# Token stage of a fused vision and text layer: filter taps stacked on the contraction rows, and four pairs of images as one run of 28 tiles

## The chip, the cores and the metric

The kernel runs on one core of a Trainium2 chip, as one program. The metric is the device time of one execution in microseconds. The profile is of one execution of the same program and lists the instructions of each engine: PE is TensorE's matmul (PEld its weight load), DVE is VectorE, ACT is ScalarE, POOL is GpSimd, and SP is SyncE, which here issues DMAs.

## The reference

Eight images of 64 channels and 56x56 pixels are turned into tokens. A patch of 3x3 taps is gathered round each pixel, gated by a small network of its own, and projected. 128 text tokens are put behind the 3136 image tokens, and one layer of causal attention (8 heads of 8, 4 key/value heads, rotary positions) and of a feed-forward block that half the tokens go through follows.

```python
t = unfold3x3(x)                                  # [8, 3136, 64*9]
h1 = relu(t @ W1 + b1)                            # 576 -> 64
s = sigmoid(h1 @ W2 + b2)                         # 64 -> 576
h = concat([(t * s) @ W3 + b3, txt], axis=1)      # 576 -> 64; [8, 3264, 64]
h = h + attention(layernorm(h), Wq, Wk, Wv, Wo)
h = h + feed_forward(layernorm(h), ...)
```

## The kernel before, in words

The program is a row of stages with a barrier between them: `tokens`, `attention`, `inverse_sums`, `second_norm`, `select` and `feed_forward`. Only `tokens` and the arrays that it reads are touched. It makes `h`, its layer norm, and queries, keys and values for attention.

**Data.** Two images form a pair: the 64 channels of each lie on 128 partitions. A loop (`Fori`) runs the pairs, four in all, and inside a pair the code runs seven tiles of 8 image rows, which are 448 tokens. Each convolution tap is a matmul of 128 contraction rows by 128 output rows by 448 columns in f32, with a block-diagonal weight: image one in one quarter, image two in the opposite one, and zeros in the other two. The trace shows an f32 matmul as two MATMUL instructions.

**One tile on PE.** Nine hidden products (`w1_sb`, L419) add up in `hidden_ps`; ACT makes `h1` of it (Relu, L469). Nine gate products (`w2_sb`, L433) go one after the other into the two slots of `gate_ps`; ACT turns each into a tanh (L475), DVE multiplies it with the shifted image (L507, `gated`), and a token product (`w3_sb`, L446) adds it into `token_ps`. Gate products are issued three ahead of the token products. When all nine are in, PE waits for its own last product and tells DVE, which takes the tile into `h0` (L492).

**What follows a tile** is called a post: `product_stage`, `activation_stage`, `vector_stage` and `sum_and_rest`. PE centres the tile (L271), ACT squares it (L303), PE averages (L275), ACT takes the root (L308), DVE the reciprocal (L324) and the normalised tile (L326). PE makes queries and keys, each once straight and once turned (L284), DVE multiplies them with cosine and sine (L338, `rot`). POOL adds the two (L371, `full`), ACT casts the sum to bf16 (L317), POOL takes the rest (L378), ACT casts that too, and POOL takes the last rest (L382): three bf16 parts, which SP stores with twelve DMAs (`store_parts`, L260). Values are made of 128 tokens at a time (L293) and copied by DVE (L355). The post of a tile is done within the tile that comes after it, at places written out by hand in `POST_AT`: centring and average between the nine hidden products, queries and keys between the gate products. The root needs another function table on ACT than tanh, so the tables are changed twice a tile (ACT_TABLE_LOAD at L308 and L475).

**Round a pair.** The text tokens are turned first (L410), and their post is put between the stages of the first tile. At the end of a pair DVE copies the next pair's images, loaded in the meantime, into the padded `x_pad` (L525); all engines meet at a barrier, SP clears the semaphores, and they meet again. The last post of a pair is done in the first tile of the next; the last of all stands behind the loop.

## Time and profile before

| | us |
|---|---|
| median of 3 runs (lowest, highest) | 5276.06 (5275.87, 5278.95) |
| the profiled execution, its own time | 5275.56 |
| its span, first to last instruction | 5274.0 |
| PE busy | 4587.6 (87%) |
| DVE busy | 4049.6 (77%) |
| ACT busy | 3538.7 (67%) |
| POOL busy | 629.6 (12%) |
| `tokens`, until the first instruction of `attention` | 928.2 |

PE is called busy from a matmul's start to its modelled end, and matmuls overlap, so sums of their durations say more than there is; the distance from one start to the next is what a matmul costs. The page gives TensorE's granted clock, of which there are two levels, 2.4 GHz (1.00) and 1.2 GHz (0.50). A timeline row merges instructions of one kind that follow each other; its second number is the time from the first's start to the last's end.

### The profile page before, as it was taken

What the parts mean: (1) busy time and instruction counts of PE and PEld (TensorE: products, weight loads), DVE (VectorE), ACT (ScalarE), POOL (GpSimd) and SP (SyncE); (2) the same over time, 40 slices, a digit from 0 to 9 for tenths busy, and PEclk for the clock granted to TensorE, in tenths of its full rate; (3) what the DMA queues carried; (4) which work ended last, traced back from release to release, by engine and by line L of the source; (5) the groups of instructions that cost most, each with busy time, mean ns of one, the idle gap of its engine ahead of it and who ended that gap; (6) DMA issues with size and microseconds to landing.
All of it is one profiled execution on the core that took longest, in us unless ns stands there. A gap on an engine that the chain in (4) does not pass through costs nothing. (4 is left out here: it accounts for less than half of the span.)

```text
span 5274.0 us, 109173 instructions
## 1 busy us (share of the span) xinstructions
PE 4587.6 (87%) x42956; PEld 1660.9 (31%) x42956; DVE 4049.6 (77%) x4595; ACT 3538.7 (67%) x7169; POOL 629.6 (12%) x1092
## 2 busy tenths in 40 slices
PE   8898987499999989999998999999899999965466
PEld 3444433133333333333333333333233333321222
DVE  5555555689989979998997999899799989965511
ACT  3343433088888878888886888888788888842133
POOL 2222222010010001001001000100100010012100
PEclk9999999599999989999998999999899999977688
DMA  3222122200010010001001000100100010024233
GB/s 109 68 68 70 56 64 61 77 15 8 8 36 8 8 31 14 8 6 37 10 6 33 12 8 6 36 10 6 35 10 8 6 38 8 6 69 140 67 105 102
DMA packets 168631, 194.27 MB, mean 37 GB/s; under 512 B 53644, under 2 KB 128572, under 8 KB 167228
## 3 DMA queue, kind: packets, MB, share of 16 engines
q1 hardware_dynamic: 168132, 187.49, 12.6%
q8 instruction: 329, 5.39, 0.4%
q14 instruction: 170, 1.39, 0.1%
HBM read 105.18 MB, written 81.36 MB: 35 GB/s over the span
## 5 line engine op out<-in xcount | busy, mean ns | idle before, releaser
L792 DVE TENSOR_REDUCE part_max<-max_scores 128x2 f32<-128x1024 f32 (+3 forms) x3096 | 3228.9, 1101 | 369.5 <-PE max_scores L750 267.0
L920 ACT ACTIVATE probs<-scores 128x512 f32<-128x512 f32 (+4 forms) x6272 | 2996.3, 538 | 547.7 <-PE scores L950 442.0
L974 PE MATMUL out_acc<-probs,v_keys 128*32 128x256 f32 (+2 forms) x23424 | 1789.8, 378 | 0.0
L750 PE MATMUL max_scores<-k_rows,q_rows 48*128 48x512 bf16 (+5 forms) x6416 | 1147.6, 370 | 184.2 <-DVE part_max L792 114.5
L950 PE MATMUL scores<-q_rows,k_rows 50*128 50x512 bf16 (+4 forms) x6272 | 1218.3, 354 | 90.3 <-ACT probs L920 45.4
L900 POOL TENSOR_SCALAR_AFFINE_SELECT probs<-probs 128x256 f32<-128x256 f32 (+1 forms) x832 | 336.1, 404 | 3418.4 <-ACT probs L920 3415.9
L750 PEld LDWEIGHTS max_scores<-k_rows,q_rows 48*128 48x128 bf16 (+1 forms) x6416 | 302.9, 94 | 1296.8 <-DVE part_max L792 757.6
L974 PEld LDWEIGHTS out_acc<-probs,v_keys 128*32 128x32 f32 x23424 | 463.0, 108 | 737.2 <-issue 624.0
L950 PEld LDWEIGHTS scores<-q_rows,k_rows 50*128 50x128 bf16 x6272 | 469.8, 94 | 434.3 <-ACT probs L920 227.5
L507 DVE SCALAR_TENSOR_TENSOR gated<-gate,x_pad 128x448 f32<-128x448 f32 x252 | 260.8, 1073 | 68.9 <-ACT gate L475 56.0
L446 PE MATMUL token_ps<-gated,w_sb 128*128 128x448 f32 x504 | 234.7, 556 | 32.9 <-DVE gated L507 32.9
L433 PE MATMUL gate_ps<-h,w_sb 128*128 128x448 f32 x504 | 231.7, 560 | 18.0 <-ACT h L469 14.5
L475 ACT ACTIVATE gate<-gate_ps,b_sb 128x448 f32<-128x448 f32 x252 | 154.9, 631 | 110.7 <-PE gate_ps L433 106.2
L324 DVE RECIPROCAL rstd<-std 128x448 f32<-128x448 f32 (+1 forms) x33 | 89.5, 2711 | 178.9 <-ACT std L308 178.9
L757 PE MATMUL max_scores<-masks_sb 64*128 64x128 bf16 (+2 forms) x3424 | 220.1, 207 | 0.0
L419 PE MATMUL hidden_ps<-x_pad,w_sb 128*128 128x448 f32 x504 | 212.9, 559 | 3.6
L1555 DVE SCALAR_TENSOR_TENSOR scaled<-y_ps,ff_b_sb,chosen 128x512 f32<-128x512 f32 (+1 forms) x28 | 19.7, 702 | 217.6 <-PE y_ps L1502 217.6
L1513 PE MATMUL hidden_ps<-normed,ff_w_sb 128*128 128x512 f32 (+1 forms) x224 | 113.9, 659 | 81.3 <-DMA chosen<-chosen_dram 81.3
L757 PEld LDWEIGHTS max_scores<-masks_sb 64*128 64x128 bf16 (+1 forms) x3424 | 163.2, 98 | 43.8 <-issue 5.1
L1542 ACT ACTIVATE hidden<-hidden_ps,ff_b_sb 128x512 f32<-128x512 f32 (+1 forms) x112 | 71.5, 649 | 150.5 <-PE hidden_ps L1513 150.5
L371 POOL TENSOR_TENSOR full<-rot 128x448 f32<-128x448 f32 (+1 forms) x66 | 69.0, 1046 | 669.2 <-DVEq L342 669.2
L446 PEld LDWEIGHTS token_ps<-gated,w_sb 128*128 128x128 f32 x504 | 88.8, 189 | 153.8 <-DVE gated L507 95.1
(122 smaller groups left out, 1980.0 us busy)
## 6 DMA issues: line engine op xcount, KB each, us to landing
q_terms_dram<-q_st SPq DMA_DIRECT2D x174, 112.0 KB
q_rows<-q_terms_dram SPq DMA_DIRECT2D x180, 96.0 KB, 2.2
v_keys<-v_blocks_dram SPq DMA_DIRECT2D x18, 832.0 KB, 9.4
v_blocks_dram<-v_st SPq DMA_DIRECT2D x26, 512.0 KB, 3.4
k_rows<-k_terms_dram SPq DMA_DIRECT2D x36, 306.0 KB, 6.7
k_terms_dram<-k_st SPq DMA_DIRECT2D x174, 56.0 KB
x_in<-in_x SPq DMA_DIRECT2D x5, 1568.0 KB, 6.1
h_dram<-h SPq DMA_DIRECT2D x28, 224.0 KB, 2.0
```

The costliest lines, as they stand in the source:

```text
L419: last = nc.tensor.matmul(hidden_ps[:, 0, 0:CT], w1_sb[:, s], x_pad[:, r0 + i:r0 + i + IMG_ROWS, j:j + W], start=(s == 0), stop=(s == SHIF ...
L433: nc.tensor.matmul(gate_ps[:, g % 2, 0:CT], w2_sb[:, s], h1[:], start=True, stop=True).then_inc(gate_ready, 1)
L446: last = nc.tensor.matmul(token_ps[:, 0, 0:CT], w3_sb[:, s], gated[:, g % GATE_RING], start=(s == 0), stop=(s == SHIFTS - 1))
L475: nc.scalar.activation(gate[:, g % GATE_RING], gate_ps[:, g % 2, 0:CT], ACT.Tanh, bias=b2_sb[:, s:s + 1], scale=0.5).then_inc(tanh_ready, 1)
L507: nc.vector.scalar_tensor_tensor(out=gated[:, g % GATE_RING].rearrange("p (h w) -> p h w", h=IMG_ROWS), in0=gate[:, g % GATE_RING].rearran ...
L750: last = nc.tensor.matmul(max_scores[to:to + m, n % M_RING, v, 0:keys], q_rows[rows, g, p, q0:q0 + m], k_rows[rows, (u // BU) % STEP_B, g, ...
L757: last = nc.tensor.matmul(max_scores[to:to + m, n % M_RING, v, keys - m + HALF * half:keys], masks_sb[rows, 1 + 2 * half, 0:m], masks_sb[r ...
L792: nc.vector.tensor_reduce(part_max[0:m, u % 2, i, :, p, c], max_scores[0:m, n % M_RING, :, 0:keys], AX_X, ALU.max).then_inc(max_used, 1)
L900: nc.gpsimd.affine_select(block_probs, block_probs, [[0, GKV], [1, keys]], ALU.is_ge, 0.0, base=0, channel_multiplier=-1).then_inc(p_maske ...
L920: nc.scalar.activation(probs[0:keys, k % P_RING, s, o:width[t]], scores[0:keys, (GH * k + s) % S_RING, o:width[t]], ACT.Exp, scale=float(H ...
L950: nc.tensor.matmul(scores[0:keys, n % S_RING, o:width[t]], k_rows[rows, u // BU, g, j * P:j * P + keys], q_rows[rows, g, p, begin[t] + o:b ...
L974: last = nc.tensor.matmul(out_acc[VW * s:VW * s + VW, lo:hi], v_keys[0:keys, u // BU, g, j, v * VW:(v + 1) * VW], probs[0:keys, k % P_RING ...
```

## The change

Everything after `tokens` is left as it is. In `tokens`:

- **Taps on the contraction rows.** Of the three taps of a filter row, the first two are stacked: `x_taps` holds, for each image, 64 channels on the lower partitions and the same channels one pixel further on the upper ones. A hidden or token product of these two taps is one matmul per image with 128 contraction rows and 64 output rows, the two images in the two halves of the output; a gate product is one per image with 64 contraction rows and 128 output rows. The third tap of each filter row stays as it was, block-diagonal for both images (`x_both`). A tile has six units: units 0 to 2 are such a couple of matmuls, units 3 to 5 one whole matmul each. The number of matmuls, tanh or sigmoid activations and gate multiplications is 9 of each as before.
- **Order.** The loop over pairs, the barriers, the clearing of semaphores and the copy into the padded image are gone; 28 tiles are written out. In a tile, unit by unit, PE issues the gates of the unit, hidden products of the next tile, token products of the unit before, and a stage of a post. A post is spread over the two tiles behind its own: `posts(n, u)` and `norms(n, u)` say what of it stands where. The text is turned in the fourth tile of a pair; its post stands there and in the fifth.
- **Gate.** The sigmoid is taken as such (L570) and not as a tanh, and DVE multiplies it with the image in a TENSOR_TENSOR (L624).
- **Loads.** The padded image comes from the host's array. SP loads it in pieces of 8 rows, five DMAs a piece, each as soon as the tile that used the old rows is done; the weights are loaded by 19 DMAs from ACT's queue.

```diff
+UNITS_T = 2 * KS
+TEXT_AT = 3
...
+        x_both = sbuf("x_both", [P, PH, PW])
+        x_taps = sbuf("x_taps", [P, 2, PH, PW])
...
+        h1 = sbuf("h1", [P, 2, CT])
...
+        def late(n):
+
+            return 1 if n % CTILES == TEXT_AT + 1 else 0
+
+        def posts(n, u):
+
+            at = []
+            if n >= 2 and u == 0:
+                at.append((POST_OF[n - 2], 3))
+            if n >= 1 and u in (1 + late(n), 2 + late(n), 5):
+                at.append((POST_OF[n - 1], {1: 0, 2: 1}.get(u - late(n), 2)))
+            if n % CTILES == TEXT_AT and u == 5:
+                at.append((text_post(n), 0))
+            if late(n) and u < 3:
+                at.append((text_post(n), u + 1))
+            return at
+
+        def norms(n, u):
+
+            if n >= 1 and u == 3 + late(n):
+                return [POST_OF[n - 1]]
+            return [text_post(n)] if late(n) and u == 0 else []
...
+        def gate_ops(u):
+            return [2 * u, 2 * u + 1] if u < KS else [KS + u]
+
+        def load_rows(eng, p, n):
+
+            r0, r1 = n * IMG_ROWS, (n + 1) * IMG_ROWS if n < CTILES - 1 else PH
+            a, b = r0 * PW, r1 * PW
+            eng.dma_start(x_both[:].rearrange("p h w -> p (h w)")[:, a:b], x[p][:, a:b]).then_inc(piece_loaded[n], 16)
+            for e in range(2):
+                flat = x_taps[:, e].rearrange("p h w -> p (h w)")
+                for half in range(2):
+                    eng.dma_start(flat[C * half:C * (half + 1), a:b],
+                                  x[p][C * e:C * (e + 1), a + half:b + half]).then_inc(piece_loaded[n], 16)
...
-        with nc.Fori(0, PAIRS) as p:
...
-                        for s in range(SHIFTS):
-                            i, j = divmod(s, KS)
-                            last = nc.tensor.matmul(hidden_ps[:, 0, 0:CT], w1_sb[:, s],
-                                                    x_pad[:, r0 + i:r0 + i + IMG_ROWS, j:j + W],
-                                                    start=(s == 0), stop=(s == SHIFTS - 1))
-                            if s in POST_AT["hidden"]:
-                                product_stage(pe, due(n), POST_AT["hidden"].index(s))
...
-            nc.all_engine_barrier(sem_only=True)
-            for s in step_sems:
-                nc.sync.sem_clear(s)
...
+                for n in range(1, NT + 1):
+                    pair, i = (n - 1) // CTILES, (n - 1) % CTILES
+                    store_h0(sp, taken_before(n - 1), pair, i * CT, CT)
+                    if pair + 1 < PAIRS:
+
+                        sp.wait_ge(hidden_ready, n)
+                        sp.wait_ge(gated_ready, SHIFTS * n)
+                        load_rows(sp, pair + 1, i)
...
+                    if u < KS:
+                        for e in range(2):
+                            last = nc.tensor.matmul(hidden_ps[C * e:C * (e + 1), 0:CT], w1p_sb[:, u],
+                                                    x_taps[:, e, r0 + u:r0 + u + IMG_ROWS, 0:W],
+                                                    start=(u == 0), stop=False, skip_group_check=True)
+                    else:
+                        row = r0 + u - KS
+                        last = nc.tensor.matmul(hidden_ps[:, 0:CT], w1b_sb[:, u - KS],
+                                                x_both[:, row:row + IMG_ROWS, 2:2 + W],
+                                                start=False, stop=(u == UNITS_T - 1), skip_group_check=True)
...
+                    for s in gate_ops(u):
+                        g = n * SHIFTS + s
+                        if g >= 2:
+                            pe.wait_ge(sigmoid_ready, g - 1)
+                        if u < KS:
+                            e = s % 2
+                            nc.tensor.matmul(gate_ps[:, g % 2, 0:CT], w2p_sb[C * e:C * (e + 1), u],
+                                             h1[C * e:C * (e + 1), n % 2], start=True, stop=True).then_inc(gate_ready, 1)
+                        else:
+                            nc.tensor.matmul(gate_ps[:, g % 2, 0:CT], w2b_sb[:, u - KS], h1[:, n % 2],
+                                             start=True, stop=True).then_inc(gate_ready, 1)
...
+                    for s in gate_ops(u):
+                        g = n * SHIFTS + s
+                        pe.wait_ge(gated_ready, g + 1)
+                        if u < KS:
+                            e = s % 2
+                            last = nc.tensor.matmul(token_ps[C * e:C * (e + 1), 0:CT], w3p_sb[:, u],
+                                                    gated[:, g % GATE_RING], start=(u == 0), stop=False,
+                                                    skip_group_check=True)
+                        else:
+                            last = nc.tensor.matmul(token_ps[:, 0:CT], w3b_sb[:, u - KS], gated[:, g % GATE_RING],
+                                                    start=False, stop=(u == UNITS_T - 1), skip_group_check=True)
+                        last.then_inc(gated_used, 1)
+                    if u == UNITS_T - 1:
+                        pe.wait_ge(gated_used, (n + 1) * SHIFTS)
+                        nc.tensor.sem_inc(token_ready, 1)
...
+                for n in range(NT):
+                    for u in range(UNITS_T):
+                        gates(n, u)
+                        if n + 1 < NT:
+                            for h in ((0, 1), (2,), (3,), (4,), (5,), ())[u]:
+                                hidden(n + 1, h)
+                        if u >= 1:
+                            if u == 1 and n % CTILES == TEXT_AT:
+                                turn_text(n)
+                            out_tokens(n, u - 1)
+                        elif n >= 1:
+                            out_tokens(n - 1, UNITS_T - 1)
+                        if u == 0:
+                            value_products(pe, n)
+                        for m, stage in posts(n, u):
+                            product_stage(pe, m, stage)
...
+                def relu(n):
+                    act.wait_ge(hidden_ready, n + 1)
+                    if n >= 2:
+                        act.wait_ge(gate_ready, (n - 1) * SHIFTS)
+                    nc.scalar.activation(h1[:, n % 2], hidden_ps[:, 0:CT], ACT.Relu, bias=b1_sb[:]).then_inc(h1_ready, 1)
...
+                for n in range(NT):
+                    for u in range(UNITS_T):
+                        if u == UNITS_T - 1 and n + 1 < NT:
+                            relu(n + 1)
+                        for s in gate_ops(u):
+                            sigmoid(n, s)
+                        for m, stage in posts(n, u):
+                            if stage <= 1:
+                                activation_stage(act, m, stage)
+                        if n >= 2 and u in (2, 4 - late(n)):
+                            activation_stage(act, POST_OF[n - 2], 2 if u == 2 else 3)
+                        if late(n) and u == 5:
+                            activation_stage(act, text_post(n), 2)
+                        if n >= 1 and late(n - 1) and u == 0:
+                            activation_stage(act, text_post(n - 1), 3)
...
+                    nc.vector.tensor_tensor(gated[:, g % GATE_RING].rearrange("p (h w) -> p h w", h=IMG_ROWS),
+                                            gate[:, g % GATE_RING].rearrange("p (h w) -> p h w", h=IMG_ROWS),
+                                            taps, ALU.mult).then_inc(gated_ready, 1)
...
+                for n in range(NT):
+                    for u in range(UNITS_T):
+                        if u == 0 and n >= 1:
+                            take_up_tile(n - 1)
+                        if u == 0:
+                            value_copies(dve, n)
+                        if u == 1 and n % CTILES == TEXT_AT:
+                            pair, t0, w, idx = POST[text_post(n)]
+                            take_up(idx, t0, w, pair)
+                        for s in gate_ops(u):
+                            gating(n, s)
+                        for m, stage in posts(n, u):
+                            if stage >= 2:
+                                vector_stage(dve, m, stage)
+                        for m in norms(n, u):
+                            vector_stage(dve, m, 1)```

How PE's order moves, first as it was: PE in one tile of the loop, from the first hidden product on (`w1_sb`, `w2_sb`, `w3_sb` are hidden, gate and token weights).

```order
L419 MATMUL hidden_ps<-x_pad,w1_sb 128x448 x2
L271 MATMUL norm_ps<-h0,centre_sb 128x448
L419 MATMUL hidden_ps<-x_pad,w1_sb 128x448 x3
L275 MATMUL norm_ps<-square,mean_sb 128x448
L419 MATMUL hidden_ps<-x_pad,w1_sb 128x448 x4
L433 MATMUL gate_ps<-h1,w2_sb 128x448 x4
L446 MATMUL token_ps<-gated,w3_sb 128x448
L284 MATMUL proj_ps<-normed,wq_sb 128x448 x2
L433 MATMUL gate_ps<-h1,w2_sb 128x448
L446 MATMUL token_ps<-gated,w3_sb 128x448
L433 MATMUL gate_ps<-h1,w2_sb 128x448
L446 MATMUL token_ps<-gated,w3_sb 128x448
```

And PE in units 0 to 2 of a tile now (`p` marks weights of stacked taps, `b` those of the third tap).

```order
L483 MATMUL gate_ps<-h1,w2p_sb 128x448 x2
L461 MATMUL hidden_ps<-x_taps,w1p_sb 64x448 x4
L511 MATMUL token_ps<-gated,w3b_sb 128x448
L307 MATMUL proj_ps<-normed,wk_sb 64x448 x2
L483 MATMUL gate_ps<-h1,w2p_sb 128x448 x2
L461 MATMUL hidden_ps<-x_taps,w1p_sb 64x448 x2
L507 MATMUL token_ps<-gated,w3p_sb 64x448 x2
L290 MATMUL norm_ps<-h0,centre_sb 128x448
L483 MATMUL gate_ps<-h1,w2p_sb 128x448 x2
L466 MATMUL hidden_ps<-x_both,w1b_sb 128x448
L507 MATMUL token_ps<-gated,w3p_sb 64x448 x2
L296 MATMUL norm_ps<-square,mean_sb 128x448
```

The nine hidden products no longer stand in a row ahead of the gates; they are those of the next tile and lie between the gates of this one, as does the last token product of the tile before.

ACT in a tile of the loop before, from the square on:

```order
L303 ACTIVATE square<-norm_ps 128x448
L308 ACT_TABLE_LOAD
L308 ACTIVATE std<-norm_ps,eps_sb 128x448
L469 ACTIVATE h1<-hidden_ps,b1_sb 128x448
L475 ACT_TABLE_LOAD
L475 ACTIVATE gate<-gate_ps,b2_sb 128x448 x6
L317 CAST q_st<-full 128x448
L317 CAST k_st<-full 64x448
L475 ACTIVATE gate<-gate_ps,b2_sb 128x448 x2
L317 CAST q_st<-rest 128x448
L317 CAST k_st<-rest 64x448
L475 ACTIVATE gate<-gate_ps,b2_sb 128x448
```

ACT now, from the Relu of the next tile (in unit 5) through units 0 to 4 of that tile:

```order
L562 ACTIVATE h1<-hidden_ps,b1_sb 128x448
L570 ACTIVATE gate<-gate_ps,b2_sb 128x448 x5
L326 ACTIVATE square<-norm_ps 128x448
L570 ACTIVATE gate<-gate_ps,b2_sb 128x448 x2
L333 ACT_TABLE_LOAD
L333 ACTIVATE std<-norm_ps,eps_sb 128x448
L341 CAST q_st<-full 128x448
L341 CAST k_st<-full 64x448
L570 ACT_TABLE_LOAD
L570 ACTIVATE gate<-gate_ps,b2_sb 128x448 x2
L341 CAST q_st<-rest 128x448
L341 CAST k_st<-rest 64x448
```

Both table loads, the root and two casts stood ahead of the first gate or between gates; now they stand in one row between the sixth gate and the seventh.

DVE now, from the taking up of a tile on; before, the reciprocal and the normalised tile stood between the taking up and the first gate multiplication:

```order
L606 TENSOR_SCALAR h0<-token_ps,b3_sb 128x448
L624 TENSOR_TENSOR gated<-gate,x_taps 128x448 x2
L360 TENSOR_TENSOR rot<-proj_ps,cos_sb 64x448
L360 TENSOR_TENSOR rot<-proj_ps,sin_sb 64x448
L624 TENSOR_TENSOR gated<-gate,x_taps 128x448 x4
L624 TENSOR_TENSOR gated<-gate,x_both 128x448
L347 RECIPROCAL rstd<-std 128x448
L349 TENSOR_TENSOR normed<-norm_ps,rstd 128x448
L624 TENSOR_TENSOR gated<-gate,x_both 128x448 x2
L360 TENSOR_TENSOR rot<-proj_ps,cos_sb 128x448
L360 TENSOR_TENSOR rot<-proj_ps,sin_sb 128x448
```

The reciprocal now stands between the seventh gate multiplication and the eighth.

## Rows read from the trace of the kernel before

**Rows 1.** Windows: stretch, us; busy us (instructions) of each engine; clock; DMA share; GB/s.
```profile
0.00:18.30 18.30, 0.45 (x1) 0.19 (x2) 8.71 (x8) 0.68 (x1) 6.31 (x6) 1.00 0.92 343
...
238.50:458.70 220.20, 197.69 (x529) 89.62 (x529) 120.28 (x141) 88.37 (x136) 54.12 (x48) 0.97 0.21 65
...
889.40:928.20 38.80, 11.99 (x32) 5.15 (x32) 10.06 (x20) 4.72 (x7) 6.21 (x6) 0.61 0.26 79
928.20:5274.00 4345.80, 3784.72 (x40816) 1297.69 (x40816) 3553.61 (x4010) 3183.22 (x6622) 400.65 (x888) 0.94 0.11 29
```

**Rows 2.** The same view for one tile of the third pair.
```profile
561.60:590.70 29.10, 27.60 (x75) 12.62 (x75) 16.52 (x17) 11.74 (x19) 7.37 (x6) 1.00 0.16 43
```

**Rows 3.** Timeline of PE there: start, duration of the merged row, idle before it.
```profile
571.02 1.72 PE L284 MATMUL proj_ps<-normed,wk_sb 128*64 128x448 f32 x4
572.67 1.02 PE L433 MATMUL gate_ps<-h,w_sb 128*128 128x448 f32 x2
...
580.31 1.02 PE L446 MATMUL token_ps<-gated,w_sb 128*128 128x448 f32 x2 [0.35 <-DVE gated L507]
581.48 1.74 PE L419 MATMUL hidden_ps<-x_pad,w_sb 128*128 128x448 f32 x4
...
586.82 3.17 PE L419 MATMUL hidden_ps<-x_pad,w_sb 128*128 128x448 f32 x8
589.83 1.89 PE L293 MATMUL proj_ps<-wv_sb,normed 128*128 128x64 f32 x16
```

**Rows 4.** Timeline of PE in attention: output rows of 32, contraction rows of 48 and 50.
```profile
2003.11 0.39 PE L750 MATMUL max_scores<-k_rows,q_rows 48*128 48x512 bf16 x2
2003.34 0.40 PE L950 MATMUL scores<-q_rows,k_rows 50*128 50x512 bf16 x2
2003.67 0.64 PE L974 MATMUL out_acc<-probs,v_keys 128*32 128x256 f32 x8
2004.24 0.39 PE L750 MATMUL max_scores<-k_rows,q_rows 48*128 48x512 bf16 x2
```

**Rows 5.** Timeline of ACT and DVE in the tile of rows 2.
```profile
560.95 0.63 ACT L469 ACTIVATE h<-hidden_ps,b_sb 128x448 f32<-128x448 f32 x1 [2.37 <-PE hidden_ps L419]
561.60 1.28 ACT L475 ACT_TABLE_LOAD   x1
562.90 1.18 ACT L475 ACTIVATE gate<-gate_ps,b_sb 128x448 f32<-128x448 f32 x2
563.56 1.18 DVE L507 SCALAR_TENSOR_TENSOR gated<-gate,x_pad 128x448 f32<-128x448 f32 x2 [1.34 <-ACT gate L475]
...
574.69 0.57 ACT L317 CAST k_st<-full 64x448 bf16<-64x448 f32 x1 [3.70 <-POOL full L371]
575.16 1.15 ACT L475 ACTIVATE gate<-gate_ps,b_sb 128x448 f32<-128x448 f32 x2
575.82 4.44 DVE L507 SCALAR_TENSOR_TENSOR gated<-gate,x_pad 128x448 f32<-128x448 f32 x3 [0.68 <-ACT gate L475]
...
587.69 2.95 DVE L324 RECIPROCAL rstd<-std 128x448 f32<-128x448 f32 x1 [5.54 <-ACT std L308]
```

**Rows 6.** Timeline of POOL and SP beside it.
```profile
576.00 1.41 POOL L378 TENSOR_TENSOR rest<-full,k_st 64x448 f32<-64x448 f32 x1
577.69 2.29 SPq L260 DMA_DIRECT2D k_terms_dram<-k_st  x3
```

**Rows 7.** Timeline of PE behind the last pair, and in `second_norm`.
```profile
897.84 1.85 PE L271 MATMUL norm_ps<-h,centre_sb 128*128 128x448 f32 x2 [8.53 <-PEq L536]
...
4725.01 2.05 PE L1244 MATMUL centred_ps<-h,centre_sb 128*128 128x512 f32 x2 [2.82 <-DVE normed L1226]
...
4765.52 2.08 PE L1236 MATMUL proj_ps<-attn,wo_sb 128*128 128x512 f32 x2 [2.96 <-POOL attn L1179]
```

**Rows 8.** Timeline of the start: SP's first issue, PE's first products.
```profile
0.82 0.40 SPq L141 DMA_DIRECT2D x_in<-in_x  x1
...
18.32 3.32 PE L419 MATMUL hidden_ps<-x_pad,w_sb 128*128 128x448 f32 x4
```

481 lines of the change are left out of this document (239 added, 242 removed).

## The prediction

> **What bounds the kernel now.** I read the windows by stage first [rows 1]. Token stage: 928.2 us, of which 18.3 are a start, 220.2 each of three pairs, 38.8 a tail with the last post, and the rest, 210.5, the last pair. The 4345.8 us behind it are untouched, so the change can only move the 928.2. Inside a pair the window over one tile [rows 2] shows PE busy 27.60 of 29.10 us at clock 1.00, DVE 16.52, ACT 11.74, POOL 7.37: PE bounds the tile.
>
> The timeline gives PE's prices [rows 3]. Eight hidden instructions take 3.17 us with 0.54 for the last one's end, so starts lie 0.376 apart and one f32 product, two instructions, costs a slot of 0.75 us. A tile has 27 + 6 = 33 products: 24.8 us; values and stalls at dependences make up the 29.1. So what is worth most is to have fewer slots.
>
> **Do two half-size products run side by side?** No f32 half product of this size is in the trace, but near ones are [rows 4]. Attention's `out_acc` is f32 with 32 output rows: four products, eight instructions of 256 columns, and the next start is 0.57 us after the first. At 0.376 per 448 columns eight in a row would be 1.72, and two 0.43. So all four lie side by side and 0.14 is lost at the change of shape. For split contraction rows there is only bf16: two `max_scores` of 512 columns, 48 rows each, and the next start is 0.23 later; 512 columns at that pace are 0.21. I take one slot for a couple, both for split outputs (near the `out_acc` row, f32) and split contractions; bounds are one and two slots. Changing shape: four key products with 64 output rows take 1.65 to the next start, against 1.50 for four instructions at that pace [rows 3]: 0.14 for a change in and one out. I take 0.1 a change, bounds 0 and 0.14.
>
> **PE's work now.** Nine couples and nine whole products plus six of the post are 24 slots, 18.0 us. The order changes shape 13 times: 1.3 us. PE's wait for its own last token product stays: 1.17 us from its start to the next [rows 3] in place of 0.75. That is 19.8 us; if PE alone set the pace, a tile would fall by 9 us. It doesn't.
>
> **The path through a tile.** ACT now has two table loads of 1.28, the root and two casts in one row between its sixth and seventh gate, and DVE a reciprocal of 2.95 between its seventh and eighth. I walk a plain tile from its first gate (0), with ACT 0.63 an activation at a pitch of 0.55, casts at a pitch of 0.47, DVE 0.63 at a pitch of 0.55 [rows 5], 0.04 to hand over, and 0.1 more where PE starts out of a wait:
> - PE: gate couple, two hidden couples, last token product with its wait, keys (two), gate couple, hidden couple, token couple, centring: ten slots, 0.42 for the wait, six changes of shape. The third gate couple starts at 8.5.
> - Its first half ends 0.92 after its start; ACT's sixth gate ends at 10.7, table load to 12.0 (PE's average, at 11.1, ends then too), root and two casts to 13.6, table load to 14.9, seventh gate to 15.6.
> - DVE: seventh multiplication to 16.2, reciprocal and normalised tile to 19.8, eighth multiplication to 20.3.
> - PE has run dry meanwhile, 0.5 us ahead of the fourth token unit and 2.6 ahead of the fifth. That starts at 20.45; with the queries (two slots) and a change of shape the next tile starts at 22.8.
>
> So 22.8 us a plain tile, 6.3 less than 29.1. Everything else has room: the casts, Relu and ninth gate end by 18.6; SP issues 12 stores at 0.76 [rows 6] and 5 loads and one more at about 0.4 [rows 8], 11.5 us in all; the loads of the next pair are due six tiles later. Gate multiplications lose their second operation and stay two SBUF inputs; I price the new form like the old.
>
> **Tiles that differ.** Eight blocks of values are 1.8 us of PE (16 instructions, [rows 3]), and keys behind them now wait for DVE's copies of the same slot: +2.2 in two tiles, +3.0 in the tile with the last blocks. Text: +1.2 in the tile that turns it (PE waits for the taking up), +2.7 in the next (another pair of table loads and a reciprocal, partly beside the values), +0.5 behind. A pair is 7 x 22.8 + 7.4 + 4.4 = 171.4 us against 220.2, and has no barrier. The first two tiles have less post: the first pair 157.
>
> **Ends.** Start: ten loads of rows and three of weights instead of everything; I take 10 us, six slots partly at half clock (1.5 us a slot, [rows 8]) and the Relu: 19 until the first gate, bounds 15 and 25. Tail: before, 30.4 us from the last centring at 897.84 [rows 7]. Now ACT casts the post before it, twice, ahead of the last square, which thus stands 8.0 behind the last token product instead of 1.9 behind the centring: 36.5.
>
> **The clock.** Within a tile before, PE was without a running matmul for 1.50 us in all, and the clock stayed at 1.00 [rows 2]. In `second_norm` it idled 2.82 and 2.96 us, and behind each gap it ran at half: matmuls of 512 columns took 2.05 and 2.08 us for two, against 1.00 at full pace, 0.43 and an end of 0.57 [rows 3, 7]. The new gap of 2.6 is nearly as long. All that PE does behind it lies on the path. Stretches at half there held some 3 to 6 us, which cost half their length. I take 1.8 us in every second tile, 25 in all; bounds 0 and 75.
>
> **Sum.** 19 + 157 + 3 x 171.4 + 36.5 + 25 = 751.7 against 928.2: 176.5 less. The profiled execution's own time is 5275.56, so 5099; the median of the runs shown is 0.5 above it. I say **5100 us**.
>
> **The rivals.**
> - *The lock between DVE and POOL.* Three multiplications beside POOL took 4.44 us instead of 1.73 [rows 5], and POOL's 1.0 became 1.41 [rows 6]. In my walk POOL is idle when the seventh and eighth run, by 0.3 us for the seventh. If both meet it, +1.8 a tile: 5150. Chance 0.10.
> - *Gate couples don't overlap.* Each half has its own wait for ACT, and f32 on split contraction rows isn't in the trace. Three slots on the path, 2.25 a tile: 5163. Against it: the bf16 `scores` have such waits too, and two of them take one's time. Chance 0.06.
> - *No couple overlaps: the change doesn't do what it says.* 33 slots again; eight couples lie ahead of the root, 5.9 a tile, and PE has no gap to lose its clock in: 5240. Against it: `out_acc`. Chance 0.04.
> - *A dearer table switch.* In the rows a switch costs the load's 1.28 and the next activation starts at once (561.60 to 562.90, [rows 5]); that is in the sum. The Trainium skill, ScalarE: Activation LUTs, in What ACT_TABLE_LOAD costs, adds a drain of about 1.38 us to each load, which no row here shows. As a mechanism: were there 1.4 us of dead time behind each load only now, when the load follows a busy ACT, two of them a tile on the path are 78 us: 5178. Chance 0.02, since the load at 561.60 follows a Relu directly too.
> - *Slower: PE stays at half clock.* If the clock falls in every gap and doesn't come back within a tile, 24 slots at 1.5 plus the rest are 38 us a tile, and with text and values the stage is near 1175: 5520. It decides from a mean tile of 30 us. Against it: at half clock PE has no gaps left in a tile, and behind each gap of `second_norm` full speed came back. Chance 0.03.
>
> **How the numbers follow.** My forecast, with the clock falling in none to all tiles and changes of shape at 0 to 0.14, is 5060 to 5130 and has 0.73; the rest, 0.02, is that some wait that I don't see eats all of it. The range goes on to take in the lock and the gate couples, and a little below for a walk that is too dear: 5050 to 5165. What a measurement here can tell from no change is 0.2%, 10.6 us. All cases but the last two are faster by more; as the walk has many steps, I leave 0.94 faster, 0.02 same, 0.04 slower.
>
> **What would show it.** Right: two halves of a couple start within some 10 ns of each other in PE's timeline, a slot of 0.75 to the next; from Relu to Relu 22 to 24 us in plain tiles; PE's longest idle time in a tile ahead of the fifth token unit, ended by DVE's `gated`; granted clock under 1.00 in the tiles; no idle time of 8.5 us between pairs. Wrong: tiles near 29 us, halves that start 0.75 apart, DVE's seventh and eighth multiplication over 1 us, PE waiting for SP's loads, or a stage behind `tokens` that takes other than 4346 us.

## The result, and the profile of the changed kernel

The changed kernel takes 5120.49 us (median of 4 runs, 5117.10 to 5121.87) against 5277.51 (5275.87 to 5283.56) of the kernel before on the same chip: a ratio of 0.9701, 95% interval 0.9689 to 0.9712. The profiled execution took 5121.87 us, its span is 5120.3. The forecast was 5100 with a range of 5050 to 5165.

The windows by stage of the changed kernel, to set beside [rows 1]. The cuts are the first gate product of the tiles 0, 7, 14 and 21, the place where a 29th tile would begin (a plain tile's 23.68 us behind the first gate of the last), and attention's first load; behind stretch and length stand busy us (instructions) of PE, PE's weight loads, DVE, ACT and POOL, then the clock, DMA share and GB/s. The last row is one plain tile, beside [rows 2].

```profile
0.00:22.94 22.94, 7.08 (x19) 2.49 (x19) 0.06 (x1) 1.92 (x2) 6.29 (x6) 1.00 0.97 265
22.94:192.88 169.94, 152.45 (x489) 55.42 (x490) 79.76 (x117) 77.84 (x123) 34.34 (x36) 0.96 0.34 96
192.88:373.05 180.17, 159.10 (x528) 57.99 (x527) 90.75 (x139) 83.51 (x134) 46.94 (x48) 0.98 0.34 100
373.05:558.13 185.08, 164.00 (x528) 60.02 (x527) 89.94 (x139) 83.51 (x134) 46.94 (x48) 0.95 0.33 97
558.13:734.56 176.43, 154.27 (x508) 56.38 (x508) 90.13 (x138) 82.99 (x133) 46.92 (x48) 0.97 0.26 77
734.56:771.80 37.24, 14.95 (x41) 6.17 (x39) 10.84 (x23) 6.87 (x11) 12.41 (x12) 0.68 0.40 125
771.80:5120.30 4348.50, 3775.99 (x40816) 1295.60 (x40816) 3552.81 (x4010) 3184.23 (x6622) 399.02 (x888) 0.94 0.11 29
...
373.05:396.73 23.68, 20.95 (x67) 7.09 (x67) 11.98 (x16) 11.37 (x18) 6.30 (x6) 1.00 0.34 98
```

The token stage is 771.8 us, 156.4 less than 928.2; the rest is 2.7 longer, 4348.5 against 4345.8. Forecast and measurement by stretch:

| | forecast | measured |
|---|---|---|
| start to the first gate | 19 | 22.94 |
| first pair | 157 | 169.94 |
| three pairs | 514.2 | 541.68 |
| stretches at half clock in the tiles | 25 | in the two rows above |
| tail | 36.5 | 37.24 |
| token stage | 751.7 | 771.80 |

Now the timeline of PE in that plain tile, beside [rows 3]: start, duration of the merged row, operation, number of instructions, idle time ahead of it and who ended it.

```profile
373.05 1.02 PE L483 MATMUL gate_ps<-h,w2p_sb 64*128 64x448 f32 x4
...
376.98 1.69 PE L307 MATMUL proj_ps<-normed,wk_sb 128*64 128x448 f32 x4 [0.30 <-PE token_ps L511]
...
379.55 0.97 PE L461 MATMUL hidden_ps<-x_taps,w1p_sb 128*64 128x448 f32 x4
380.36 0.92 PE L507 MATMUL token_ps<-gated,w3p_sb 128*64 128x448 f32 x4
381.21 1.02 PE L290 MATMUL norm_ps<-h,centre_sb 128*128 128x448 f32 x2
382.16 1.02 PE L483 MATMUL gate_ps<-h,w2p_sb 64*128 64x448 f32 x4
383.11 1.02 PE L466 MATMUL hidden_ps<-x_both,w1b_sb 128*128 128x448 f32 x2
384.06 0.97 PE L507 MATMUL token_ps<-gated,w3p_sb 128*64 128x448 f32 x4
384.96 1.02 PE L296 MATMUL norm_ps<-square,mean_sb 128*128 128x448 f32 x2
385.82 0.92 PE L486 MATMUL gate_ps<-h,w2b_sb 128*128 128x448 f32 x2
...
394.28 1.02 PE L511 MATMUL token_ps<-gated,w3b_sb 128*128 128x448 f32 x2 [2.28 <-DVE gated L624]
```

A couple of half products is four instructions, and its halves start some 7 ns apart. It takes a slot: from the hidden couple at 379.55 to the token couple of the same shape at 380.36 it is 0.81 us, from that to the next row 0.85, each with a change of shape on one side. What a change costs is shown by products that have one on both sides: the gate couple at 382.16 and the whole product at 383.11 take 0.95 each, the mean at 384.96 takes 0.86 up to a gate of its own shape, and that gate takes 0.75 (to 386.57, a whole product again). So a change of shape is 0.2 us, about half of it in the product ahead and half in the one behind. The third gate couple starts 9.11 us behind the first (382.16 - 373.05), the fifth token unit 21.23 behind it, after PE's longest idle time of the tile, 2.28 us, which DVE's `gated` ends.

ACT and DVE in the same tile; the first row holds the fifth and the sixth gate:

```profile
383.21 1.16 ACT L570 ACTIVATE gate<-gate_ps,b_sb 128x448 f32<-128x448 f32 x2 [0.40 <-PE gate_ps L483]
384.38 1.28 ACT L333 ACT_TABLE_LOAD   x1
386.02 0.63 ACT L333 ACTIVATE std<-norm_ps,eps_sb 128x448 f32<-128x448 f32 x1 [0.35 <-PE norm_ps L296]
386.55 0.56 ACT L341 CAST q_st<-full 128x448 bf16<-128x448 f32 x1
387.00 0.56 ACT L341 CAST k_st<-full 64x448 bf16<-64x448 f32 x1
387.58 1.28 ACT L570 ACT_TABLE_LOAD   x1
388.88 1.16 ACT L570 ACTIVATE gate<-gate_ps,b_sb 128x448 f32<-128x448 f32 x2
```

```profile
389.55 0.62 DVE L624 TENSOR_TENSOR gated<-gate,x_both 128x448 f32<-128x448 f32 x1 [4.51 <-ACT gate L570]
390.09 2.94 DVE L347 RECIPROCAL rstd<-std 128x448 f32<-128x448 f32 x1
393.07 0.62 DVE L349 TENSOR_TENSOR normed<-norm_ps,rstd 128x448 f32<-128x448 f32 x1
393.61 1.15 DVE L624 TENSOR_TENSOR gated<-gate,x_both 128x448 f32<-128x448 f32 x2
```

That is the row that the forecast walked: gate, table, root, casts, table, gate, multiplication, reciprocal, normalised tile, multiplication, and then PE's fifth token unit. The seventh and eighth multiplication take 0.62, not the 1.48 each of three in [rows 5]: POOL isn't beside them.

### The profile page after: what moved, and what is told of

Read it like the earlier page. It is cut to its first block and busy times, and to the rows that moved or that the text cites. A ratio compares the mean times of both kernels' runs of the same rounds, so it can differ in the third digit from the quotient of the medians.

```text
span 5120.3 us, 108154 instructions
## 1 busy us (share of the span) xinstructions
PE 4427.8 (86%) x42924; PEld 1534.1 (30%) x42924; DVE 3914.3 (76%) x4567; ACT 3520.9 (69%) x7159; POOL 592.9 (12%) x1086
## 5 line engine op out<-in xcount | busy, mean ns | idle before, releaser
L570 ACT ACTIVATE gate<-gate_ps,b_sb 128x448 f32<-128x448 f32 x252 | 148.1, 631 | 285.9 <-PE gate_ps L483 265.3
L624 DVE TENSOR_TENSOR gated<-gate,x_taps 128x448 f32<-128x448 f32 x168 | 107.2, 680 | 89.4 <-ACT gate L570 86.9
L624 DVE TENSOR_TENSOR gated<-gate,x_both 128x448 f32<-128x448 f32 x84 | 53.2, 656 | 129.4 <-ACT gate L570 129.4
L511 PE MATMUL token_ps<-gated,w3b_sb 128*128 128x448 f32 x168 | 89.3, 614 | 61.1 <-DVE gated L624 58.2
L1327 PE MATMUL proj_ps<-attn,wo_sb 128*128 128x512 f32 (+1 forms) x56 | 42.1, 844 | 103.8 <-POOL attn L1270 103.8
L1309 DVE RECIPROCAL rstd<-std 128x512 f32<-128x512 f32 (+1 forms) x28 | 85.8, 3065 | 47.4 <-ACT std L1253 47.3
```

Source lines behind the costliest of these rows:

```text
L511: last = nc.tensor.matmul(token_ps[:, 0:CT], w3b_sb[:, u - KS], gated[:, g % GATE_RING], start=False, stop=(u == UNITS_T - 1), skip_group_ ...
L570: nc.scalar.activation(gate[:, g % GATE_RING], gate_ps[:, g % 2, 0:CT], ACT.Sigmoid, bias=b2_sb[:, u:u + 1]).then_inc(sigmoid_ready, 1)
L624: nc.vector.tensor_tensor(gated[:, g % GATE_RING].rearrange("p (h w) -> p h w", h=IMG_ROWS), gate[:, g % GATE_RING].rearrange("p (h w) -> ...
L1309: nc.vector.reciprocal(rstd[:, m % 2, 0:w], std[:, m % 2, 0:w]).then_inc(rstd_ready, 1)
```

## Experiments

What each was to tell: how much is the order and how much the stacking (order_alone); whether the row on ACT and DVE sets the tile, and from which point (casts_later, tight_slot, loose_slot, norm_behind); what the idle time does to the clock (fill_gap); the price of a change of shape and of PE's wait for itself (tight_slot, keys_whole, no_drain); and what a version without that row on the path gives (norm_behind, best, best2). Each ratio is against the kernel before, with its 95% interval. The edits are abridged: lines are shortened, and flags and helpers left out.

### The order without the stacking: order_alone

```diff
-for e in range(2): matmul(hidden_ps[C*e:C*(e+1), 0:CT], w1p_sb[:, u], x_taps[:, e, ...])
+for e in range(2): matmul(hidden_ps[:, 0:CT], w1b_sb[:, u], x_taps[:, e, ...])
-matmul(gate_ps[:, g % 2, 0:CT], w2p_sb[C*e:C*(e+1), u], h1[C*e:C*(e+1), n % 2])
+matmul(gate_ps[:, g % 2, 0:CT], w2b_sb[:, u], h1[:, n % 2])
-matmul(token_ps[C*e:C*(e+1), 0:CT], w3p_sb[:, u], gated[:, g % GATE_RING])
+matmul(token_ps[:, 0:CT], w3b_sb[:, u], gated[:, g % GATE_RING])
```

> The new order is kept, and each of the nine couples of half products in a tile becomes two whole products of 128 x 128 with the weights of a single shift (the values that it computes are not the reference's): 33 products a tile again, as in the kernel before, and hardly a change of shape. Theory 1 (couples share PE's time; stacking is what shortens the tile): in the changed kernel's plain tile of 23.68 us PE works or waits on itself 21.1; nine products of 0.75 more and some eleven changes of shape of about 0.18 less are 25.8, and 1 to 3 us of stalls, so 27 to 29 us a tile; no idle time of 2.28 ahead of the fifth token unit, granted clock 1.00 in the tiles; time 5190 to 5250, and what is missing to 5277.5 is what the order alone gives (30 to 90 us). Rival (the order without barriers gives nearly all, since ACT and DVE set the tile anyway): tiles under 25 us, 5120 to 5145.

Measured: 5253.55 us, 0.9958 (0.9942 to 0.9973). That is 3.6 above the expectation. Of the 157 us that the change saves, all that isn't stacking (the order, the run without barriers, the new gate and the loads, which this experiment doesn't tell apart) gives some 22 (14 to 31 by the interval), and the stacking the other 135. PE's timeline in a plain tile:

```profile
285.59 1.02 PE L511 MATMUL token_ps<-gated,w3b_sb 128*128 128x448 f32 x2 [2.28 <-DVE gated L624]
...
287.95 1.67 PE L483 MATMUL gate_ps<-h,w2b_sb 128*128 128x448 f32 x4
...
300.69 1.67 PE L483 MATMUL gate_ps<-h,w2b_sb 128*128 128x448 f32 x4
...
313.67 1.02 PE L511 MATMUL token_ps<-gated,w3b_sb 128*128 128x448 f32 x2 [2.28 <-DVE gated L624]
```

A couple is now two products in a row, 1.50 us, and the third pair of gates starts 12.74 behind the first (300.69 - 287.95) where the stacked kernel has 9.11; a tile takes 28.1 (313.67 - 285.59). The theory on the couples holds, and the size agrees with the forecast's rival in which no couple overlaps (5240). One thing that both it and the expectation said is wrong: PE's idle time of 2.28 us is still there, and the clock still falls. The row behind the sixth gate bounds this order with 33 slots as with 24; stacking pays because most of the couples lie ahead of that row.

### The row made shorter: casts_later

```diff
-if n >= 2 and u in (2, 4 - late(n)):
-    activation_stage(act, POST_OF[n - 2], 2 if u == 2 else 3)
+if n >= 2 and u in ((2, 3) if late(n) else (3, 5)):
+    activation_stage(act, POST_OF[n - 2], 2 if u == 3 - late(n) else 3)
```

> The two casts of the high parts leave ACT's row between its sixth and seventh gate and stand behind the seventh; the two of the middle parts move from behind the eighth to behind the ninth. Theory 1 (the row of table load, root, two casts, table load on ACT and the reciprocal on DVE sets when the fifth token unit starts): the two casts held 1.03 us of the row, so that unit starts 1.03 earlier, PE's idle time ahead of it goes from 2.28 to 1.25 us, the plain tile from 23.68 to 22.65, and the clock no longer falls in plain tiles: 28 us from the row and 10 to 18 from the clock, 5075 to 5095. Rival 1 (PE's own work sets the tile, and the wait is only where its slack shows): 5115 to 5121. Rival 2 (POOL's subtractions, which follow the casts, now meet DVE's seventh and eighth multiplication, and each of them takes about 1 us longer): the gain is given back, 5110 to 5150, and gated multiplications over 0.75 us on average.

Measured: 5084.65 us, 0.9644 (0.9631 to 0.9658). The timelines of PE, DVE and POOL in a plain tile:

```profile
232.59 1.02 PE L483 MATMUL gate_ps<-h,w2p_sb 64*128 64x448 f32 x4
...
252.91 1.02 PE L511 MATMUL token_ps<-gated,w3b_sb 128*128 128x448 f32 x2 [1.78 <-DVE gated L624]
...
255.36 1.02 PE L483 MATMUL gate_ps<-h,w2p_sb 64*128 64x448 f32 x4
```

```profile
248.72 2.95 DVE L347 RECIPROCAL rstd<-std 128x448 f32<-128x448 f32 x1
...
252.24 1.99 DVE L624 TENSOR_TENSOR gated<-gate,x_both 128x448 f32<-128x448 f32 x2
```

```profile
248.67 1.04 POOL L403 TENSOR_TENSOR rest<-full,q_st 128x448 f32<-128x448 f32 x1 [8.25 <-ACT q_st L341]
...
252.33 1.41 POOL L407 TENSOR_TENSOR q_st<-rest,q_st 128x448 bf16<-128x448 f32 x1 [1.64 <-ACT q_st L341]
```

The plain tile is 22.77 us (255.36 - 232.59): 0.91 off, of the 1.03 that the casts held. PE's idle time is 1.78 and not the 1.25 of the expectation, since PE, too, comes 0.4 earlier: the wait ahead of the fourth token unit is gone. In plain tiles the clock no longer falls; seven stretches at half are left of twelve, all in or behind the tiles behind the text's. Both together shorten the token stage by 33.2 us (738.6 in place of 771.8), of the 36 between the medians. Rival 2 came true in a place where it costs nothing: the eighth and ninth multiplication now take 1.99 together instead of 1.15, with POOL's second subtraction beside them, but it is the ninth that is late, and nobody waits for that one yet.

### A slot ahead of the sixth gate, and one behind it: tight_slot, loose_slot

Two kernels that give PE more to do, in two places.

```diff
 # tight_slot: first hidden couple
-for e in range(2): matmul(hidden_ps[C*e:C*(e+1), 0:CT], w1p_sb[:, 0], x_taps[:, e, ...])
+for e in range(2): matmul(hidden_ps[:, 0:CT], w1b_sb[:, e], x_taps[:, e, ...])
 # loose_slot: third token couple
-for e in range(2): matmul(token_ps[C*e:C*(e+1), 0:CT], w3p_sb[:, 2], gated[:, ...])
+for e in range(2): matmul(token_ps[:, 0:CT], w3b_sb[:, e], gated[:, ...])
```

> Only the first hidden couple of each tile becomes two whole products (weights of other shifts: the values are not the reference's). It stands ahead of the sixth gate, from which the row on ACT starts. One slot of 0.75 us more, and one change of shape more (whole to couple). Theory 1 (a slot ahead of the sixth gate lies on the path; a change of shape costs 0.2): 0.96 a tile, plain tiles of 24.64, the idle time ahead of the fifth token unit still 2.28, and 27 tiles of it: 5146. With the 0.1 a change that the forecast took: 24.54 and 5143. Rival (PE has slack there too, as the row waits for something else): under 23.9 a tile, 5120 to 5127.

> Only the third token couple of each tile (the one between the eighth gate and the fifth hidden product) becomes two whole products (with the weights of other shifts: the values are not the reference's). From the changed kernel's timeline that is 1.88 us from the hidden product ahead of it to the next gate in place of 1.37: PE gets 0.51 us more work a tile. Theory 1 (behind the sixth gate the row on ACT and DVE sets the end, PE has slack): the fifth token unit starts as before, 21.1 to 21.2 us behind the first gate, the plain tile stays at 23.68, the idle time ahead of that unit falls from 2.28 to about 2.07, and with less idle time the clock may fall less often: 5105 to 5121, not slower for all that it does more. Rival (PE's work sets the tile): 0.51 x 28 = 14 us more, 5135.

Measured: tight_slot 5157.42 us, 0.9774 (0.9760 to 0.9787); loose_slot 5122.88, 0.9713 (0.9700 to 0.9726). PE's timeline of a plain tile of tight_slot (the whole products are at 256.72), and then of one of loose_slot (at 259.48):

```profile
255.77 1.02 PE L488 MATMUL gate_ps<-h,w2p_sb 64*128 64x448 f32 x4
256.72 1.77 PE L461 MATMUL hidden_ps<-x_taps,w1b_sb 128*128 128x448 f32 x4
...
280.39 1.02 PE L488 MATMUL gate_ps<-h,w2p_sb 64*128 64x448 f32 x4
```

```profile
245.21 1.02 PE L483 MATMUL gate_ps<-h,w2p_sb 64*128 64x448 f32 x4
...
259.48 1.67 PE L511 MATMUL token_ps<-gated,w3b_sb 128*128 128x448 f32 x4
...
266.44 1.02 PE L514 MATMUL token_ps<-gated,w3b_sb 128*128 128x448 f32 x2 [2.28 <-DVE gated L627]
...
268.89 1.02 PE L483 MATMUL gate_ps<-h,w2p_sb 64*128 64x448 f32 x4
```

The tile of tight_slot is 24.62 us long (280.39 - 255.77), 0.94 more than 23.68: one slot of 0.75 and one change of shape of 0.2, as theory 1 has it, and not the 0.1 of the forecast. The tile of loose_slot is 23.68 (268.89 - 245.21), though PE has 0.51 us more work in it: the rival (5135) is out, and theory 1 holds. Its time is 1.9 above that theory's range, and one of its details doesn't hold: the idle time of 2.28 is as long as before, since the 0.51 us were taken ahead of the fourth token unit, where a wait of 0.3, a change of shape and a start out of a wait fell away, and not ahead of the fifth. So the clock fell no less.

tight_slot's total is 11 us above what was expected. The clock is why: from the second tile to the last but one 19 stretches of 3.41 us are at half speed, in the changed kernel 12, and seven more at 1.6 (below) are 11 us. loose_slot has 14. Each of these two has one more in the first tile.

### The idle time and the clock: fill_gap

```diff
+if u == UNITS_T - 1 and n >= 1:
+    for k in range(9):
+        matmul(token_ps[:, CT:CT + 64], centre_sb[:], centre_sb[:, 0:64], start=True, stop=True)
```

> Nine more products of 64 columns with constants, some 2.0 us of PE, stand ahead of each tile's fifth token unit, where PE idles 2.28 us; their results go to columns that nothing reads. Theory 1 (the idle time is what takes the clock down, and each stretch at half costs about 1.5 us): the stretches at half clock behind that idle time are gone from the tiles (8 of 12; the four tiles behind the text's have another idle time, ahead of the queries, of 2.50 us, and keep theirs), 12 us less: 5105 to 5110. Rival 1 (the falls hit work that has slack): 5119 to 5122. Rival 2 (the filling delays the fifth token unit): tiles of 23.7 to 24.5, 5120 to 5140.

One thing the expectation left out: the fill begins a sum of its own in the bank in which the token units of the tile are being summed, and the tokens that this kernel computes aren't the reference's. The Trainium skill, PSUM — Partial Sum Buffer, in PSUM: the matmul accumulator, says that such a start clears the marks of the whole bank; no run here shows it by itself. Measured: 5103.42 us, 0.9677 (0.9664 to 0.9690). The windows of one tile, the seventh of the second pair, in the changed kernel, with its idle time and what came behind it:

```profile
345.64:373.05 27.41, 24.76 (x83) 9.31 (x82) 13.43 (x20) 11.36 (x18) 6.30 (x6) 0.94 0.34 105
366.65:368.93 2.28, 0.00 (x0) 0.00 (x0) 2.25 (x4) 0.63 (x1) 0.59 (x1) 1.00 0.53 138
369.64:373.05 3.41, 3.41 (x5) 1.01 (x3) 0.62 (x1) 0.00 (x0) 0.00 (x0) 0.50 0.19 56
```

and in fill_gap, window and PE's timeline:

```profile
336.79:362.54 25.75, 25.05 (x102) 11.04 (x101) 13.42 (x20) 11.37 (x18) 6.31 (x6) 1.00 0.37 113
```

```profile
357.64 2.12 PE L529 MATMUL token_ps<-centre_sb 128*128 128x64 f32 x18
360.08 1.02 PE L512 MATMUL token_ps<-gated,w3b_sb 128*128 128x448 f32 x2 [0.33 <-DVE gated L629]
```

With the fill the same tile is 1.66 us shorter and the granted clock 1.00; without it, PE idles 2.28 us, and 0.71 us after it works again it runs at 1.2 GHz in place of 2.4 for 3.41 us. Ahead of the last tile one such stretch is left of twelve, and from the first gate to where a 29th tile would begin it is 693.8 us in place of 711.6: 1.6 us a stretch, about half its length. Theory 1 holds; the gain is 17 us, not 12, because the tiles behind the text's, where an idle time of 2.50 is now one of 2.00, keep their clock too, in three of four cases.

### PE's wait for itself and the shape of the keys: no_drain, keys_whole

```diff
 # no_drain
-pe.wait_ge(gated_used, (n + 1) * SHIFTS); pe.sem_inc(token_ready, 1)
-dve.wait_ge(token_ready, idx + 1)
+dve.wait_ge(gated_used, (pair * CTILES + t0 // CT + 1) * SHIFTS)   # text: token_ready, pair + 1
 # keys_whole
-matmul(proj_ps[0:rows, n % 2, 0:w], w_sb[:, turned], normed[:, t0:t0 + w])
+matmul(proj_ps[:, n % 2, 0:w], wq_sb[:, turned], normed[:, t0:t0 + w])
```

> The changed kernel, where PE no longer waits for the end of its own last token product before it tells DVE: DVE's taking up waits itself for the count of used gated tiles. In the changed kernel's timeline that product's second instruction is followed by the first key product 1.02 us later, where 0.376 and a change of shape of 0.06 would do: 0.58 a tile. Theory 1 (everything ahead of the sixth gate is on the path): third gate couple 8.5 us behind the first in place of 9.1, plain tile 23.1, 16 us less, 5104. Rival (DVE's taking up, the gate multiplications behind it or the second gate couple set that part of the tile): third gate couple at 8.9 to 9.1, 5115 to 5121.

> The two key products write 128 rows with the queries' weights in place of 64 with the keys' own (the key values are not the reference's): the same columns and instructions, but the change of shape between the last token product and the keys is gone, one of 13 in a tile. It stands ahead of the sixth gate. A price of 0.2 a change: third gate couple 8.9 us behind the first in place of 9.1, plain tile 23.48, the token stage 5 us shorter. A price of 0.1, as the forecast had it: 9.0, 23.58, 3 us. If not the change of shape but the half products themselves are dearer than a slot: 9.1, 23.68, nothing.

no_drain: 5116.80 us, 0.9711 (0.9692 to 0.9730), not to be told from the changed kernel by its time. Its third gate couple starts 8.76 behind the first and the plain tile is 23.33: 0.35 off, half-way between the theories. The expectation had misread its row: the keys' first product starts 0.84 behind that second instruction, not 1.02, and without a wait 0.47 is left, half a change of shape among it. So the wait costs 0.35 a tile, 9 us in all; the stage is 7.6 shorter, 1.3 of it by a sooner first gate, with 14 stretches at half clock in place of 12 (counted as above).

keys_whole: 5121.68 us in one run, plain tile 23.73, third gate couple at 9.16. It looks like the third case, but doesn't show it: in its timeline the change of shape it was to remove lies in PE's wait for the token product (0.30 us in both kernels) and cost nothing there. It was the wrong change to take away; the price was settled by tight_slot.

### The row off the path: norm_behind, best, best2

```diff
 # norm_behind, on top of casts_later
-if n >= 2 and u == 0: at.append((POST_OF[n - 2], 3))
-if n >= 1 and u in (1 + late(n), 2 + late(n), 5): ...
+if n >= 2 and u in (0, 1): at.append((POST_OF[n - 2], 2 + u))      # queries, then keys
+if n >= 1 and u in (1 + late(n), 2 + late(n)): ...
-if n >= 1 and u == 3 + late(n): return [POST_OF[n - 1]]             # reciprocal
+if n >= 1 and u == (3 if n % CTILES == TEXT_AT else 5): return [POST_OF[n - 1]]
 # best, on top: the last tile's reciprocal, the tail's order on PE and ACT, a table load at the start
+if n >= 1 and u == (3 if n % CTILES == TEXT_AT or n == NT - 1 else 5): return [POST_OF[n - 1]]
+for post, stage in ((m, 0), (m, 1), (m - 1, 2), (m - 1, 3), (m, 2), (m, 3)): activation_stage(...)
+activation(warm[:], eps_sb[:], ACT.Sigmoid)
 # best2, on top: no_drain's edit, and
+if n >= 1 and u == (3 if n % CTILES == TEXT_AT or n == NT - 1 else 4): return [POST_OF[n - 1]]
```

> Besides the casts of the run casts_later, the reciprocal and the normalising multiplication stand behind the ninth gate multiplication (in the text's tile they stay), and the queries and keys of a post are multiplied in the first two units of the tile after. Theory 1 (with the reciprocal off the way to the fifth token unit nothing but PE's own work bounds a tile): that unit starts some 17.5 us behind the tile's first gate in place of 21.2, PE idles under 1 us anywhere, the clock stays at 1.00, a plain tile takes 20.5 to 21.5 us: 60 to 105 us less than the changed kernel, 5015 to 5060. Rival 1 (the keys wait for DVE's copies of the queries, which now stand in the same unit, or the next gate waits behind the reciprocal): a new idle time of 1 to 2 us a tile in the first two units, 5065 to 5110. Rival 2 (the row on ACT alone is enough to hold the tile): plain tile 22.65 as in casts_later, and no gain over it.

> The kernel of the run norm_behind with its ends mended. Its tail from the last tile's first gate is 66.4 us, where casts_later has 57.6: the last post's square stood behind four casts of the post before it on ACT. Now PE centres the last post right behind the queries of the one before, ACT squares it and takes the root ahead of those casts, and the last tile has its reciprocal behind the seventh gate multiplication again. At the start one sigmoid of a single column is run ahead of everything, so that the table is loaded while the first rows come in. Theory (the two ends are on the path): tail 57 to 59 us, first gate at 21.6 and first sigmoid 2.6 us earlier, so 9 to 12 us less than norm_behind: 5038 to 5043. Rival (in the tail POOL's twelve operations of about 1 us and the stores set the end): the tail stays above 63, 5045 to 5049.

> The kernel of the run best with the same edit as no_drain, and with the reciprocal behind the eighth gate multiplication in place of the ninth, so that the queries don't wait for the normalised tile either. In best PE's only idle time in a plain tile of 21.09 us is 0.56 ahead of the queries. Theory 1 (PE's own work is the bound there): that idle time goes, 20.5 us a tile, 13 to 16 us less than best: 5023 to 5027. Rival (the ninth gate multiplication, now behind the reciprocal, comes too late for the last token product): that product waits 0.3 us or more, tiles of 20.8 to 21.1, 5031 to 5040.

| run | us | ratio (95%) | plain tile |
|---|---|---|---|
| changed kernel | 5120.49 | 0.9701 (0.9689 to 0.9712) | 23.68 |
| casts_later | 5084.65 | 0.9644 (0.9631 to 0.9658) | 22.77 |
| norm_behind | 5050.97 | 0.9575 (0.9561 to 0.9590) | 21.09 |
| best | 5039.32 | 0.9557 (0.9543 to 0.9570) | 21.09 |
| best2 | 5031.90 | 0.9536 (0.9522 to 0.9550) | 20.71 |

PE's longest idle time in a plain tile of best, and of best2:

```profile
219.76 1.77 PE L308 MATMUL proj_ps<-normed,wq_sb 128*128 128x448 f32 x4 [0.56 <-DVE normed L350]
```

```profile
214.40 1.02 PE L512 MATMUL token_ps<-gated,w3b_sb 128*128 128x448 f32 x2 [0.37 <-DVE gated L628]
```

With the reciprocal behind the ninth multiplication the idle time of 2.28 is gone, PE's own work and 0.56 us of waiting are the tile, and theory 1 of norm_behind has the tile's length right (its 17.5 us to the fifth token unit forgot that queries and keys now stand ahead of it: 20.25). The ends: best's tail from the last tile's first gate is 59.9 us, one or two more than expected, and its first gate is 2.6 earlier, of which 0.9 are rows that came in sooner; 11.6 us less than norm_behind, as the theory said. best2 shows its rival: the reciprocal now makes the ninth multiplication late, the last token product waits 0.37 us, the tile is 20.71, and the gain on best, 7 us, is too small for the intervals, which overlap. By the medians the two are 81 and 89 us faster than the changed kernel.

## Why the prediction was right, and where it was off

**What it had right.** The kind of bound: stacking takes PE off the path, and what then sets a tile is ACT's two table loads, root and casts with DVE's reciprocal behind them. The order of that row, its idle time (2.6 forecast, 2.28 measured, ahead of the fifth token unit and ended by `gated`), the shorter one ahead of the fourth (0.5 and 0.3), the tail (36.5 and 37.24), and the rest of the program (4345.8 and 4348.5). Both kinds of couple take one slot. For the split contraction that was less sure than the forecast's reading of [rows 4] makes it: at the pace of [rows 3] 512 columns are 0.43 us and not 0.21, and no row there has one such product alone. The clock's term was 25 us, from 1.8 in every second tile; it was twelve stretches in 28 tiles at 1.6, 19 us. That the share came out near is luck: no row gave it, and why it is so stays open.

**Where its 20 us went.** The step that failed is a price: "I take 0.1 a change, bounds 0 and 0.14". It came from the keys' own row, 1.65 in place of 1.50 [rows 3], but the products beside them pay as well. In the kernel before, the gate behind the keys starts at 572.67, and its next product is

```profile
573.53 0.91 PE L446 MATMUL token_ps<-gated,w_sb 128*128 128x448 f32 x2
```

0.86 behind it, where 0.75 would do; the token product ahead of the keys takes 0.95, 0.1 of which is its start out of a wait. That makes 0.34 for the change in and the one out, where the forecast counted 0.14. The changed kernel shows 0.2 a change, tight_slot too. Six changes ahead of the third gate couple make its 8.5 into 9.11. Second, PE's average, forecast to start at 11.1 and to end with the table load, starts at 11.91 (384.96), and the root waits 0.35 for it behind the load, where the forecast had no wait. Together they move the fifth token unit from 20.45 to 21.23 and the plain tile from 22.8 to 23.68. The text's tile and the values' were right to within 0.5 us on top of that. With twelve stretches of 1.6 taken out, the four pairs hold 692.4 us and the forecast's 671.2: 21 us too little. The third miss is the start: ten loads were to be in after 10 us, and PE's first product is released by `x_taps` at 13.70:

```profile
13.70 4.62 PE L461 MATMUL hidden_ps<-x_taps,w1p_sb 128*64 128x448 f32 x12 [13.70 <-DMA x_taps<-in_x]
```

That is 3.7 of the 3.9. The clock gives 6 back, and 4 + 21 - 6 + 1 are the 20.

**The rivals.** No lock of DVE and POOL in the two multiplications that count, 0.62 each; casts_later brings it about, in the ninth. Gate couples overlap. No table switch has dead time behind it: the load at 387.58 ends at 388.86 and the gate starts at 388.88. No couple overlapping would have been 5253.55 where the rival said 5240; its remark that PE then has no idle time was wrong. PE didn't stay at half clock: behind each stretch of 3.41 us full speed came back.

**What stays open.** Why the clock falls at the end of, or right behind, seven of the 21 idle times of 2.28 us in the changed kernel and not at the other 14. Four of the five other stretches stand at the idle times of 2.50 in the tiles behind the text's, and one, in a tile with values, behind 0.58 us, 9.5 us after the 2.28 of the tile before:

```profile
403.77:407.18 3.41, 3.41 (x6) 0.91 (x6) 2.87 (x12) 0.00 (x0) 0.00 (x0) 0.50 0.45 131
```

From kernel to kernel the number differs (12 in the changed one, 14 in loose_slot and no_drain, 19 in tight_slot, with the same idle time), and with it a total by up to 11 us that no wait of the program explains.

## What to carry to other kernels

When a change makes the bounding engine cheaper, walk one whole tile over all engines before dividing anything: here PE lost nine slots, 6.75 us, and the tile 5.4, and the next bound, a row of table loads and a reciprocal in the order of two other engines' programs, could be moved off the path by nothing but the order, for another 70 us (norm_behind); with the ends and PE's wait for itself it was 89. A slot is worth its time only ahead of the point where that row starts: a couple made whole cost 0.94 us a tile there, and behind it, where it was 0.51 us of work, nothing. Where half products are mixed with whole ones, count the changes of shape, and take their price with the products on both sides, where none of them waits.

## What the runs showed of the hardware that was not expected

- A change of shape on PE costs 0.2 us at 448 columns of f32, spread over the products on both sides (0.95 for a couple or a whole product between two of other shapes, 0.81 to 0.86 with a change on one side, 0.75 between equal ones). The Trainium skill, TensorEngine Tiling (Array Packing), in Key Properties, says that a change of mode drains the engine. The trace has a cost at each change, as that would make it, but doesn't show the drain itself.
- At the end of, or right behind, 7 of 21 idle times of 2.28 us and all four of 2.50 the clock was granted at half, each time for 3.41 us. In casts_later, with 1.78, it was 1.00 in all plain tiles; but behind the idle time of 1.78 that norm_behind, best and best2 keep in the text's tiles it fell in one, two and three of four.
- POOL's subtraction beside the reciprocal made neither longer (1.04 and 2.95 us); beside a gate multiplication, which reads two tensors of SBUF (casts_later), the multiplication took 1.46 and the subtraction 1.41.
